# Attention scores from stacks of rounded queries and keys in a decoder layer, with the feed-forward normalisation on GpSimd

## The reference

```
x = x + attention(layernorm(x))          # 16 heads of 8 channels, causal softmax, rotary factors
x = x + cross_attention(layernorm(x), ctx)   # one head of 128 channels, no mask
x = x + ffn(layernorm(x))                # router picks 2 of 8 experts a token, plus a gated shared expert
```

## Time and profile before

| | us |
|---|---|
| median of 3 runs | 451.53 (450.38 to 453.11) |
| the profiled execution, its own time | 452.42 |
| its span, first to last instruction | 450.6 |
| busy PE / DVE / ACT / POOL | 421.9 / 343.3 / 302.2 / 210.3 |
| mean granted TensorE clock | 0.98 |

### The profile page before, as it was taken

How to read it: one execution, slowest core, us unless ns; L and a number is a source line. 1 busy time by engine, 2 the same in 40 slices (tenths; PEclk the granted TensorE clock), 3 DMA queues, 4 the chain that set the end, 5 groups by cost and what they waited for, 6 DMA issues and landing times.

```text
span 450.6 us, 13716 instructions
## 1 busy us (share of the span) xinstructions
PE 421.9 (94%) x4498; PEld 289.8 (64%) x4498; DVE 343.3 (76%) x1183; ACT 302.2 (67%) x986; POOL 210.3 (47%) x259
## 2 busy tenths in 40 slices
PE   8788999999999999999999998789999999999991
PEld 6434555556556556556565556478788888888781
DVE  7546677898898898897887866895677777777476
ACT  3455778888788788788798885765556555555420
POOL 7860030212434432532323336577466666676563
PEclk9998999999999999999999997989999999999998
DMA  7400111011021011111111106322333333332196
GB/s 202 128 27 20 43 55 51 20 56 56 21 63 57 14 55 59 37 45 50 43 52 33 33 21 178 120 74 65 77 100 91 90 96 88 94 93 71 59 353 190
DMA packets 42006, 34.70 MB, mean 77 GB/s; under 512 B 6481, under 2 KB 36961, under 8 KB 41937
## 3 DMA queue, kind: packets, MB, share of 16 engines
q1 hardware_dynamic: 36782, 24.38, 18.8%
q0 software_dynamic: 4320, 8.99, 5.9%
q10 hardware_dynamic: 834, 0.46, 0.4%
HBM read 17.26 MB, written 12.09 MB: 65 GB/s over the span
## 4 chain that ended last, share of the span: by engine, by line
PE 78%; DVE 10%; ACT 5%; issue 4%; POOL 3%; POOLq 0%; DVEq 0%; ACTq 0%
PE ps_scores L953 11%; PE ps_scores L740 8%; PE ps_shared L970 7%; PE ps_shared L791 7%; PE ps_scores L773 6%; PE ps_scores L876 4%; PE ps_shared L961 4%; PE ps_scores L769 3%; PE ps_shared L842 3%; PE ps_shared L717 3%; ACT probs L1085 3%; PE ps_scores L778 2%; PE ps_shared L912 2%; PE ps_shared L848 2%; PE ps_shared L831 2%
## 5 line engine op out<-in xcount | busy, mean ns | idle before, releaser
L647 POOL DMA_INDIRECT ys<-ctx_t,xload x71 | 68.8, 969 | 37.6 <-ACT ctx_t L1201 33.3
L630 POOL TENSOR_TENSOR x1b<-x,bias 128x128 f32<-128x128 f32 x32 | 14.5, 453 | 146.7 <-DVE x L1323 146.7
L1085 ACT ACTIVATE probs<-ps_scores 128x512 f32<-128x512 f32 x128 | 69.8, 608 | 15.8 <-PE ps_scores L778 15.8
L624 POOL DMA_INDIRECT xs<-xrow,posu x64 | 64.6, 1010 | 26.8 <-issue 13.7
L953 PE MATMUL ps_scores<-wide,xe 128*128 x213 | 66.8, 422 | 0.7 <-DVE xe L1508 0.7
L1300 DVE TENSOR_REDUCE negmax<-ps_scores 128x4 f32<-128x512 f32 x64 | 41.1, 683 | 11.0 <-PE ps_scores L747 10.4
L1079 ACT ACTIVATE s_copy<-ps_scores 128x512 f32<-128x512 f32 x64 | 38.4, 605 | 14.0 <-PE ps_scores L747 13.8
L1519 DVE COPY probs<-ps_shared 128x256 f32<-128x256 f32 x71 | 30.1, 424 | 22.1 <-PE ps_shared L961 22.1
L970 PE MATMUL ps_shared<-wd,probs 128*128 x284 | 43.4, 275 | 0.1
L740 PE MATMUL ps_scores<-wide,qk 32*128 32x512 f32 x256 | 37.1, 649 | 3.2 <-ACT probs L1085 3.1
L1300 DVE TENSOR_REDUCE negmax<-s_copy 128x4 f32<-128x512 f32 x64 | 40.0, 666 | 0.0
(11 more groups left out here) (241 smaller groups left out, 1017.1 us busy)
## 6 DMA issues: line engine op xcount, KB each, us to landing
xload<-xs SPq DMA_DIRECT2D x71, 66.0 KB, 1.9
wide<-ys SPq DMA_DIRECT2D x8, 512.0 KB, 8.9
wide<-qk SPq DMA_DIRECT2D x62, 64.0 KB, 1.9
ctx_t<-in_ctx SPq DMA_DIRECT2D x32, 64.0 KB, 1.9
out_x<-res SPq DMA_DIRECT2D x8, 256.0 KB, 3.9
ys<-ctx_t,xload POOLq DMA_INDIRECT x71, 2.3
wd<-in_L_ffn_w_down SPq DMA_DIRECT2D x8, 128.0 KB, 2.3
xs<-xrow,posu POOLq DMA_INDIRECT x64, 2.4
```

The lines of the kernel that those rows point to most:

```text
L624: pool.indirect_dma_start(out=xs, out_offset=bass.IndirectOffsetOnAxis(ap=posu[:, g % 2, k, u:u + 1], axis=0), in_=xrow[:, g % 2, k, u, :] ...
L647: pool.indirect_dma_start(out=ys, out_offset=bass.IndirectOffsetOnAxis(ap=xload_i[:, i % XL, C + 1:C + 2], axis=0), in_=ybuf[:, i % 4, :], ...
L1085: act.activation(probs[:, b % 2, j * HJ:(j + 1) * HJ, :].rearrange("p a t -> p (a t)"), SC[score_bank(("scores_t", b), j)][:], ACT.Exp)\
```

## The change

- `scores` and `scores_t` take both operands from stacks. For every head 24 of 32 rows hold q and k in three terms: rounded k with rounded q, the rest of k with rounded q, rounded k with the rest of q. The row at offset 31 of each 32-row strip holds ones in `k_stack` and the negated maximum in `q_stack`, so the transposed product takes the maximum in by itself; `scores` leaves that row out. Each burst is 16 fp32r products of 32 (31) rows with 128 columns and a weight load each, in place of four (eight) of 512 columns.
- The rounded part and the rest are made by POOL (`heads`: a copy and a subtraction of 128x512, for k and for q of each group); for the first group by ACT and DVE. SP's `place` moves them in six DMAs of 128 rows of 2 KB a group (before: eight of 32 rows); the first group is placed in twelve, six for its first sequence (three each on SP and ACT) and six for the other three.
- The maxima's DMA goes straight into row 31 of the q stacks; it may run up to six sequences ahead of the last reader instead of one.
- `norm_ffn` moves from DVE to POOL, behind that slot's scatters.
- `route` sheds the four chained additions for one sum over the group and one addition behind the weights; `ranks` adds three small matmuls instead. The gates' exponentials and additions are done once, at the last group (`gates`).
- `ORDER`, `BANK` and the bank waits are new; the depth of the pipeline from `scores` to `router` stays seven slots.

```diff
 ORDER = {
...
     "POOL": [
-        ("scatter", -3, 0, None),
-        ("weights", -24, None, None),
-        ("attn_out", 6, None, None),
-        ("norm_x", 16, None, 0),
-        ("scatter", -3, 1, None),
+        ("heads", 35, 1, 0),
+        ("weights", -1, None, None),
+        ("norm_x", 39, None, 0),
+        ("scatter", 20, 0, None),
+        ("heads", 36, 0, 0),
+        ("attn_out", 29, None, None),
+        ("scatter", 20, 1, None),
+        ("norm_ffn", 27, None, None),
     ],
...
     "ACT": [
+        ("exps", -6, 0, None),
+        ("turn_x2", -9, None, None),
+        ("exps", -6, 2, None),
+        ("exps", -6, 1, None),
+        ("turn_max", -5, None, None),
+        ("exps", -6, 3, None),
...
+            def place(g, part):
+                if g == 0:
+                    if part == 0:
+                        first_stacks()
+                    return
+                n, low, target, source = stack_move(g, part, range(GB))
+                w.ge((heads_hi, heads_lo)[low][n], g + 1)
...
+                sp.dma_start(target, source).then_inc(placed[n][g % 2], 16)
...
+            def heads(g, n):
...
+                w.ge(placed[n][(g - 1) % 2], 16 * 3 * ((g + 1) // 2))
+                pool.tensor_copy(heads_hl[:, n, 0], qk[:, g % 2, 1 - n]).then_inc(heads_hi[n], 1)
+                w.ge(heads_hi[n], g + 1)
+                pool.tensor_tensor(heads_hl[:, n, 1], qk[:, g % 2, 1 - n], heads_hl[:, n, 0].bitcast(fp32), ALU.subtract)\
+                    .then_inc(heads_lo[n], 1)
...
+            def norm_ffn(b):
+                g, u = b // GB, b % GB
+                w.ge(x2_rstd, b + 1)
+                w.ge(scattered[g % 2][u], 16 * 2 * (g // 2))
+                pool.tensor_scalar(xrow[:, g % 2, 0, u, 0:C], res[:, b, :], mv3[:, 0:1], rs3[:, 0:1], ALU.subtract, ALU.mult)\
+                    .then_inc(xn3_ready, 1)
...
             def scores(b):
...
-                for j in range(NJ):
-                    r = slice(32 * j, 32 * (j + 1))
-                    pe.matmul(bank[j][:], qk[r, g % 2, 0, ts], k_heads[r, g % 2, :, ts], start=True, stop=True)
+                for i in range(HJ):
+                    for j in range(NJ):
+                        r = slice(32 * j, 32 * j + 31)
+                        pe.matmul(bank[j][:, i * T:(i + 1) * T], q_stack[r, g % 2, i, ts], k_stack[r, g % 2, i, ts],
+                                  start=(i == 0), stop=(i == HJ - 1), skip_group_check=True)
...
             def scores_t(b):
...
-                for j in range(NJ):
-                    pe.matmul(bank[j][:], one_row4[32 * j:32 * j + 1, :], max_row[32 * j:32 * j + 1, b % 2, :], start=True, stop=False)
-                pe.wait_ge(q_placed[g % 2], 16 * HJ * (g // 2 + 1))
-                for j in range(NJ):
-                    r = slice(32 * j, 32 * (j + 1))
-                    pe.matmul(bank[j][:], qk[r, g % 2, 1, ts], q_heads[r, g % 2, :, ts], start=False, stop=True)
+                for i in range(HJ):
+                    for j in range(NJ):
+                        r = slice(32 * j, 32 * (j + 1))
+                        pe.matmul(bank[j][:, i * T:(i + 1) * T], k_stack[r, g % 2, i, ts], q_stack[r, g % 2, i, ts],
+                                  start=(i == 0), stop=(i == HJ - 1), skip_group_check=True)
...
+            def first_stacks():
+                for n in range(2):
+                    w.bank_read(("project", 0, n))
+                    act.activation(heads_hl[:, n, 0], qk[:, 0, 1 - n], ACT.Copy).then_inc(heads_hi[n], 1)
+                for part in (1, 3, 4):
+                    n, low, target, source = stack_move(0, part, range(1))
...
+                    act.dma_start(target, source).then_inc(first_placed, 16)
...
-                for u in range(GB):
-                    nxt = cum[:, p, u + 1, :] if u + 1 < GB else cum[:, 1 - p, 0, :]
-                    ins = dve.tensor_tensor(nxt, cum[:, p, u, :], selb[:, u, :], ALU.add)
-                    if u + 1 < GB:
-                        rstep(ins)
-                ins.then_inc(ranked, 1)
...
-                dve.tensor_scalar(cwg[:, g * GB:(g + 1) * GB].rearrange("p (u a) -> p u a", a=1), mx9[:, :, E:NE], 1.0, None, ALU.add)
-                rstep(dve.reduce_sum(rsum[:], mx9[:, :, 0:E], axis=AX.X))
+                rstep(dve.reduce_sum(rsum[:], top_exp[:], axis=AX.X))
...
+                    rstep(dve.reduce_sum(chosen32[:], selb[:].rearrange("p u e -> p e u"), axis=AX.X))
+                    dve.tensor_tensor(cum[:, 1 - p, :], cum[:, p, :], chosen32[:], ALU.add)
```

More of the change, by code:

```diff
@@ L94 @@
-        ("turn_max", -3, None, None),
-        ("turn_xprobs", -8, None, None),
+        ("scores", -4, None, None),
+        ("project", -1, 0, 0),
+        ("xscores", -9, None, None),
+        ("values", -6, None, None),
+        ("project_v", -3, None, None),
+        ("scores_t", -5, None, None),
+        ("turn_ffn", -11, None, None),
+        ("xout", -10, None, None),
+        ("turn_x2", -8, None, None),
+        ("router", -11, None, None),
+        ("tall_sums", -6, None, None),
+        ("turn_max", -4, None, None),
@@ L129 @@
-        ("attn_out", -3, None, None),
-        ("tall_sums", -2, None, None),
-        ("norm_x_stats", 8, None, 0),
-        ("turn_x", 1, None, 0),
-        ("norm_ffn", -6, None, None),
-        ("route", -10, None, 0),
-        ("ranks", -11, None, 0),
-        ("project", 3, 0, 0),
-        ("project", 3, 1, 0),
-        ("norm_xattn", -3, None, None),
-        ("row_max", 1, 0, None),
+        ("split", -35, None, None),
+        ("row_max", 1, 1, None),
+        ("xscores", -4, None, None),
@@ new lines @@
+        ("turn_xprobs", -5, None, None),
+        ("project", 4, 0, 0),
+        ("row_max", 1, 3, None),
+        ("turn_x", 2, None, 0),
+        ("norm_xattn", -3, None, None),
+        ("row_max", 1, 2, None),
+        ("xout", -5, None, None),
+        ("router", -6, None, None),
+        ("tall_sums", -1, None, None),
+        ("attn_out", -2, None, None),
+        ("ranks", -10, None, 0),
+        ("norm_x_stats", 9, None, 0),
+        ("route", -9, None, 0),
+        ("project", 4, 1, 0),
@@ L146 @@
 EARLY_HI = {("turn_ffn", 28): 2, ("turn_ffn", 30): 2, ("rstd_ffn", 31): 1, ("turn_ffn", 31): 2}
-EARLY_LO = {("norm_ffn", 30): 2, ("norm_ffn", 31): 1}
-GROUP_STAGES = ("norm_x_stats", "rstd_x", "norm_x", "turn_x", "project", "route", "ranks")
+EARLY_LO = {("router", 29): 2, ("router", 30): 1}
+GROUP_STAGES = ("norm_x_stats", "rstd_x", "norm_x", "turn_x", "project", "heads", "place", "route", "ranks")
 ENTRIES = [entry for entries in ORDER.values() for entry in entries]
@@ L635, in weights @@
                 pool.iota(padrow_i[:, :, C + 1], pattern=[[T, E + SPARE]], base=TRASH, channel_multiplier=1).then_inc(pad_ready, 1)
-            w.run("POOL", {"norm_x": norm_x,
+            w.run("POOL", {"norm_x": norm_x, "heads": heads, "norm_ffn": norm_ffn,
                    "attn_out": attn_out, "scatter": scatter, "weights": weights})
@@ L1417, in ranks @@
                 rstep(dve.reduce_sum(posf[:], sel[:], axis=AX.X))
-                dve.wait_ge(route_step, ahead[0])
                 dve.tensor_copy(posu[:, p], posf[:]).then_inc(drain, 1)
```

208 lines of the change are left out of this document (109 added, 99 removed).

## The result

| | before | after |
|---|---|---|
| median of the runs, us | 451.85 (450.38 to 453.11) | 444.06 (443.12 to 444.86, 4 runs) |
| profiled execution / its span | 452.42 / 450.6 | 444.36 / 442.6 |
| mean granted TensorE clock | 0.98 | 0.943 |

What follows compares the result with a forecast made beforehand. PE bounded the steady part (98.7% busy), DVE and ACT close behind; after the change ACT would be longest. 452.4 - 24.8 (steady) + 1.5 (start) - 1.5 (first slots) + 1.0 (end) = 427.6, said as 428; range 415 to 446 us.

Steps and rivals of the forecast that it cites:

- The bursts: PE in `scores` and `scores_t`: 0.11 us a round, 0.5 a burst, eight bursts replacing 9.5 us a group.
- Rivals 1 (bursts of 0.9): PE's bursts: a round costs 0.22 us, steady period 30.0, total about 441 us; chance 0.15.
- 5 (above 1.2): PE's loads not side by side: 1.8 us a burst, total 484; chance 0.10 with start and end costs together.
- The two ends: Outside the steady part: start +1.5 us, first four slots -1.5, end +1.5 for `norm_ffn` and -0.5 for `route`.
- rival 3: Granted clock falls in the steady part, once a group costing about 1.7 us, 11 in all: 440; chance 0.05.
- the prediction's own sign: Prediction is wrong if the steady group is outside 27.2 to 30.2 us or the ends move over 4 us.
- The steady sum: Steady group of four sequences: ACT longest at 27.0 us, taken as 95.5% busy, so 28.3; saves 24.8 us.
- Contention: DVE held up by POOL's streaming work in the steady part: 0.5 to 1 us a group, DVE 26.5.
- POOL's heavy slot: Steady part: 9 us of POOL work in a slot of 7, costed at nothing; without cover 2 us a group.
- Rival 2: New wait, POOL's heavy slot or maxima's DMA behind the stacks: 1.5 to 2 us a group, 440; chance 0.13.
- norm_ffn: Four norms of 0.332 us leave DVE for POOL, taking 1.33 us a group off DVE.
- The tail: Stretch from `scores` 31 to the last `router`: +1.0 us, with `norm_ffn` behind scatters +1.5 and `route` -0.5.

Runs made afterwards that it cites:

- turns_two: Changed kernel with 28 more idle transposes ahead of the first `scores` and 20 ahead of the first `turn_max`: 480.77 us, ratio 0.9989 to kernel before.
- control: The changed kernel itself, unedited, run again on another chip beside kernel before: 492.23 us, ratio 1.0284 to kernel before.
- max_unmasked: Changed kernel without the causal mask in `scores`, so maxima are taken over all keys: ratio 1.0012 to kernel before; steady group 28.57 us against 29.36.
- norm_late_dve: Changed kernel with `norm_ffn` of sequences 27 to 31 back on DVE, the others on POOL: ratio 1.0116 to kernel before.

## Why the prediction was right and wrong

**The bursts** took 0.60 us instead of 0.50, a round 0.15, between the 0.11 and 0.22 that were the bounds; whether load and product overlap within a strip isn't shown by it, nor by the row that the prediction took for it, which has the spacing of 0.11 and not what fills it. PE's 9.5 us a group became 8 x 0.6 = 4.8, not 4.0. Rivals 1 (bursts of 0.9) and 5 (above 1.2) are out.

**The two ends** failed most. "The first four slots are bound by the score chain ... -1.5, bounds 0 and -5.5" is the wrong step: it took durations at full clock. I had read the earlier trace rows, where the clock fell behind a pause of PE, and priced the clock as rival 3 in the steady part alone, where it then stood at 1.00. At the start I costed the pause (+1.5, measured +2.0), but not what it brings: at the lower clock those slots took 6.6 us more than before, and turns_two, with both pauses bridged, starts the fifth sequence 8.7 us ahead of control. Bridged, the start is near the forecast's net 0 (42.41 against 41.38, a start of kernel before that had 3.4 us at half clock itself). This is the larger part of the 16 us missing: 8.6, with 6.5 in the steady part. By the prediction's own sign, ends that move by more than 4 us, it was wrong; that the time still lies in the range owes to the width of the range. (Its chances for forecast and rivals 1 to 3 add up to 0.85, not 0.82.)

**The steady sum**: "I take 95.5% of ACT, 28.3". Measured 29.4, ACT 88% busy and PE 97%, where I had said above 94% and below 95%. The group sums of engines were fair for DVE (26.5, measured 26.7) and ACT (27.0, 25.9), low for PE (26.4, 28.6) and POOL (19.1, 20.5). The wrong step is to take the longest engine's sum for the bound: the slots are of four kinds (6.8 to 8.25 us), and pieces of 0.2 to 0.3 us added on PE, ACT or DVE cost them nearly nothing. In the long slot the trace shows a chain over PE and DVE; for the others one is argued, not shown. Of the 1.1 us, the bursts' 0.8 count by some 0.45, if they count as max_unmasked's (0.8 of 1.44, an estimate); the rest is that step. It is 6.5 us over the stage.

**Contention** was costed at 0.5 to 1 us of DVE's time and **POOL's heavy slot** at nothing. DVE's sum came out near it (26.7), and a group is 29.36 us without scatters and 29.39 with them, so neither shows in the period. The Trainium skill (SBUF — State Buffer, SBUF: two separate sides) has one of DVE and GpSimd blocked for the whole instruction of the other. The trace agrees in kind: DVE's other norm, 338 ns in the middle, took 0.65 to 0.99 us eight times of 32, and each time ended 0.02 to 0.09 us behind a POOL instruction. Rival 2's waits don't show in the steady part; the stacks' DMAs landed after 2.5 us (3.9 assumed). **norm_ffn** off DVE was worth 1.2 us a group, near its 1.33.

**The tail** came as said, +1.2 for +1.0, but norm_late_dve doesn't bear out the cause I gave, so the number is luck as far as is known. What the late norms cost on the other chips lies behind the last router, where the forecast was 0.

## What to carry to other kernels

Where a change delays the first work of TensorE, price the clock behind the pause, not the pause alone, and fill it with idle matmuls up to the last wait of the start: one bridged of two gave under half (3.3 of 8.7 us). For a steady part in a fixed order over several engines, follow the chain from start to start in each kind of slot; sums of busy time give only a lower bound, and a piece of work costs what it adds at its own place. Compare such kernels on more than one chip, as 2.8% slower and 1.7% faster were both true. And cut the whole span into stretches when an edit is judged: norm_late_dve gained nothing where it was looked for, and its 5.5 us stood in the next stretch.

## What the runs showed of the hardware

Three things were not expected. The granted clock stood at half for about 30 us behind a pause of 3 us, in one kernel, and for some 10 us behind 4 us in the other. On four of five chips kernel before was 6% slower; where it was traced, ACT and DVE started over 0.5 us late behind PE in 29 of 284 steps of the expert tiles, and records of semaphore updates were missing (50 for 71 instructions of one line), which looks like lateness if it is counted from them. And GpSimd's 128x128 `tensor_scalar` with two operands from memory took 0.80 us, against 0.46 for its addition of the same size.
